# A gated cross-attention kernel on one Trainium2 core: the score operands' stacks filled inside SBUF instead of through DRAM, and the split of the negated maxima moved from VectorE to GpSimd

## The reference

```
x = x + tanh(g_xattn[0]) * xattn(layernorm(x), ctx, Wq, bq, Wk, bk, Wv, bv, Wo, bo)
x = x + tanh(g_ffn[0])   * ffn(layernorm(x), gate_up_packed, gate_up_scales, down_packed, down_scales)

# xattn: channels are split in 8 heads of 16, the 512 columns are the sequence
q, k, v = Wq x + bq, Wk c + bk, Wv c + bv        # per batch 128 x 512
q, k = rope(q, 8), rope(k, 8)                    # the first 8 channels of each head are rotated
p = softmax(q^T k / 4)                           # per head 512 x 512
out = Wo (p v) + bo
```

## Time and profile before

| | us |
|---|---|
| median of 3 runs | 924.72 (924.64 to 926.47) |
| the profiled execution: its time | 918.37 |
| its span | 916.6 |
| PE, DVE, ACT, POOL busy | 815.8, 522.1, 483.6, 178.5 |
| mean granted TensorE clock | 0.945 of full speed |

### The profile page before, as it was taken

One profiled execution on the slowest core, in us unless ns is written; L12 is line 12 of the kernel. 1 busy time (PEld: TensorE's weight loads), 2 busy tenths in 40 slices (PEclk: granted clock), 3 DMA queues, 4 the chain that ended last, 5 costly groups with the idle time before them and its releaser, 6 DMA issues. The chain is left out here.

```text
span 916.6 us, 13653 instructions
## 1 busy us (share of the span) xinstructions
PE 815.8 (89%) x5110; PEld 421.6 (46%) x5142; DVE 522.1 (57%) x760; ACT 483.6 (53%) x895; POOL 178.5 (19%) x174
## 2 busy tenths in 40 slices
PE   3378999999998988999993599999999999999997
PEld 1123333333333333334332376666666666666664
DVE  4398977888987867888871961314131423141113
ACT  2227776887787766778792552325231623252223
POOL 1232333333333423331112820000000000000000
PEclk8559999999999988999996889999999999999999
DMA  5678555666665666465212010002000110000001
GB/s 167 171 198 218 155 142 153 189 200 194 170 165 152 175 175 189 119 167 153 69 33 79 8 46 1 1 1 67 25 1 1 47 45 0 0 27 21 0 1 46
DMA packets 55176, 86.44 MB, mean 94 GB/s; under 512 B 19274, under 2 KB 20938, under 8 KB 55114
## 3 DMA queue, kind: packets, MB, share of 16 engines
q1 hardware_dynamic: 55114, 85.62, 33.0%
HBM read 44.70 MB, written 34.34 MB: 86 GB/s over the span
## 5 line engine op out<-in xcount | busy, mean ns | idle before, releaser
L670 DVE TENSOR_REDUCE neg_max<-s_ps 128x2 f32<-128x1024 f32 x256 | 310.0, 1219 | 61.8 <-PE s_ps L420 60.8
L536 ACT ACTIVATE probs<-st_ps 128x512 f32<-128x512 f32 x512 | 277.9, 597 | 105.5 <-PE st_ps L432 101.2
L448 PE MATMUL pv_ps<-probs,v_ones 128*32 128x256 f32 x2048 | 166.1, 397 | 12.6 <-ACT pv_sb L542 12.6
L1098 PE MATMUL gu_ps<-x_head,gu_head 128*128 128x512 f32 x352 | 155.9, 443 | 0.0
L965 DVE TENSOR_TENSOR hidden<-gu_ps,silu 128x512 f32<-128x512 f32 x44 | 30.4, 691 | 202.6 <-ACT silu L1040 202.6
L420 PE MATMUL s_ps<-k_stack,q_stack 48*128 48x512 f32 x512 | 135.4, 526 | 10.5 <-DVE neg_max L670 8.4
L1099 PE MATMUL gu_ps<-x_rest,gu_head 128*128 128x512 f32 x352 | 139.0, 395 | 0.0
L1040 ACT ACTIVATE silu<-gu_ps 128x512 f32<-128x512 f32 x44 | 26.3, 597 | 204.8 <-PE gu_ps L1101 204.8
L432 PE MATMUL st_ps<-q_stack,k_stack 50*128 50x512 f32 x512 | 110.6, 421 | 12.9 <-DMA q_stack<-max_scratch 12.7
L420 PEld LDWEIGHTS s_ps<-k_stack,q_stack 48*128 48x128 f32 x512 | 50.4, 193 | 121.1 <-issue 81.1
L1115 PE MATMUL y_ps<-dn_head,h_head 128*128 128x512 f32 x176 | 101.5, 577 | 1.1 <-DVE h_rest L967 1.0
(11 more groups left out here) (114 smaller groups left out, 807.1 us busy)
## 6 DMA issues: line engine op xcount, KB each, us to landing
q_stack<-image SPq DMA_DIRECT2D x64, 192.0 KB, 3.9
k_stack<-image SPq DMA_DIRECT2D x64, 192.0 KB, 4.5
image<-split_head SPq DMA_DIRECT2D x32, 256.0 KB
image<-split_head SPq DMA_DIRECT2D x64, 128.0 KB
image<-split_rest SPq DMA_DIRECT2D x32, 256.0 KB
ct<-ctx_dram SPq DMA_DIRECT2D x16, 256.0 KB, 5.5
swap<-proj SPq DMA_DIRECT2D x64, 64.0 KB, 2.0
scale_of<-inverse_scratch SPq DMA_DIRECT2D x16, 256.0 KB
```

The costliest lines, as they stand in the source:

```text
L448: last = nc.tensor.matmul(pv_ps[2 * KC * j:2 * KC * (j + 1), cols], v_ones[b % 2][:, kt, j, quad, :], probs[at % PROBS][:, j, cols], start ...
L536: nc.scalar.activation(probs[at % PROBS][:, tile % 4, :], st_ps[item % ST_BANKS][:], ACT.Exp).then_inc(st_read, 1)
L670: nc.vector.tensor_reduce(neg_max[j // 2][:, :, j % 2, qt], s_ps[item % S_BANKS][:], AXIS_X, ALU.max, negate=True).then_inc(s_read, 1)
L1098: nc.tensor.matmul(gu_ps[t % 2][:, half], head, x_head[:, k], start=(k == 0), stop=False)
```

## The change

`image` goes. `swap` and `turned` become 128 x 2 x 512 and cover q and k as whole tiles: the tables of cosine and sine have ones and zeros for channels that are not rotated, and `by_cosine`, `by_sine` and `split_rests` on GpSimd work on 1024 elements a partition. `split_heads` is one cast of 1024 elements on DVE at slot 4. The stacks (now three of them, q and k in one tile) are filled by `build_stacks`: six DMAs from `split`, each from 64 partitions to 16. The projections are q and k with all 128 columns, after slots 9 and 12; v's is at slot 5. The maxima's head and rest are made by `split_max` on GpSimd, and the transposes stand after slot 11 (`h = 0`, before: 7) and slot 1 (`h = 1`, before: 0). `merge_quads` is one DMA (before: four), `store_inverse` one (two), `load_inverse` two (one).

```diff
-X_TILES, C_TILES, PROBS = 8, 4, 3
-MIX_AT, ROT_AT, PASS_AT, V_AT = 1, 2, 5, 8
+X_TILES, C_TILES, PROBS, STACKS = 8, 4, 3, 3
+MIX_AT, HEADS_AT, V_AT, Q_AT, K_AT = 1, 4, 5, 9, 12
+Q_REST, Q_HEAD, K_HEAD, K_REST = range(4)
+BLOCKS = ((Q_HEAD, K_HEAD), (Q_HEAD, K_REST), (Q_REST, K_HEAD))
...
+            def fill_stacks(sp, n, blocks):
+                stack = stacks[n % STACKS]
+                for at in blocks:
+                    q, k = BLOCKS[at]
                     for odd in two:
+                        rows = stack[STACK * odd + KC * at:STACK * odd + KC * (at + 1)].bitcast(F32)
+                        pair = split[STACK * odd:STACK * (odd + 1), q:k + 1:k - q, :].bitcast(F32)
+                        sp.dma_start(rows.rearrange("c j w t -> c (j w t)"), pair).then_inc(stack_in[n % STACKS], 16)
+
+            def build_stacks(sp, n):
+                if n >= STACKS:
+                    sp.wait_ge(st_full, last_weight(n - STACKS, 1))
+                sp.wait_ge(heads, n + 1)
+                fill_stacks(sp, n, (0,))
+                sp.wait_ge(rests, n + 1)
+                fill_stacks(sp, n, (1, 2))
...
             def sync_step(sp, b):
-                nxt, proj_n = b + 1 < B, b + AHEAD_PROJ
-                if nxt:
-                    load_half(sp, b + 1, 1)
+                nxt = b + 1 < B
                 store_max(sp, b, 1)
-                if proj_n < B:
-                    swap_partners(sp, proj_n)
                 if b:
                     gather_sums(sp, b - 1, 1)
+                load_max(sp, b, 1)
+                if b:
                     merge_quads(sp, b - 1)
-                load_max(sp, b, 1)
-                if b >= 2:
-                    store_x(sp, b - 2)
-                if b:
                     store_inverse(sp, b - 1)
-                if proj_n < B:
-                    store_head(sp, proj_n, 1)
                 if b + 2 < B:
-                    load_half(sp, b + 2, 0)
+                    build_stacks(sp, b + 2)
                 if nxt:
                     store_max(sp, b + 1, 0)
                 if b:
                     load_inverse(sp, b - 1)
-                if proj_n < B:
-                    store_rest(sp, proj_n, 1)
-                if b + 5 < B:
-                    load_inputs(sp, b + 5)
+                if b + 4 < B:
+                    load_inputs(sp, b + 4)
                 if nxt:
                     load_max(sp, b + 1, 0)
+                if b >= 2:
+                    store_x(sp, b - 2)
                 gather_sums(sp, b, 0)
-                if proj_n < B:
-                    store_head(sp, proj_n, 0)
-                    store_rest(sp, proj_n, 0)
+                if b + AHEAD_PROJ < B:
+                    swap_partners(sp, b + AHEAD_PROJ)
...
+            def split_max(pool, n, h):
+                pool.wait_ge(s_read, S_NO["score", n, (h + 1) * SLOTS // QUADS - 1] + 1)
+                if n:
+                    pool.wait_ge(max_line[h], n)
+                maximum = neg_max[h][:].rearrange("p o j k -> p (o j k)")
+                nc.gpsimd.tensor_copy(max_rows[h][:, 0], maximum).then_inc(max_head[h], 1)
+                pool.wait_ge(max_head[h], n + 1)
+                nc.gpsimd.tensor_tensor(max_rows[h][:, 1], maximum, max_rows[h][:, 0].bitcast(F32), ALU.subtract).then_inc(max_rest[h], 1)
...
             def pool_step(pool, b):
+                split_max(pool, b, 1)
+                if b + 2 < B:
+                    by_sine(pool, nc.gpsimd, b + 2)
+                if b + AHEAD_PROJ < B:
+                    normalise(pool, nc.gpsimd, b + AHEAD_PROJ)
+                if b + 2 < B:
+                    split_rests(pool, nc.gpsimd, b + 2)
+                if b + 1 < B:
+                    split_max(pool, b + 1, 0)
                 if b >= 2:
                     residual(pool, nc.gpsimd, b - 2)
-                if proj_n < B:
-                    rotate(pool, nc.gpsimd, proj_n)
-                    rest_pass(pool, nc.gpsimd, proj_n)
-                if b + 4 < B:
-                    normalise(pool, nc.gpsimd, b + 4)
-                if proj_n < B:
-                    rest_rot(pool, nc.gpsimd, proj_n)
                 if b:
                     scale_heads(pool, nc.gpsimd, b - 1)
+                if b + AHEAD_PROJ < B:
+                    by_cosine(pool, nc.gpsimd, b + AHEAD_PROJ)
```

More of the change, by code:

```diff
@@ L120, in attend @@
         proj = sb("proj", [P, 2, T], F32)
[L121 to L127, removed]
+        swap, turned = sb("swap", [P, 2, T], F32), sb("turned", [P, 2, T], F32)
+        split = sb("split", [P, 4, T], F32R)
+        stacks = [sb(f"stacks{n}", [P, PAIRS, 2, T], F32R) for n in range(STACKS)]
+        v_ones = [sb(f"v_ones{p}", [P, KT, QUAD, V_WIDTH], F32) for p in two]
         probs = [sb(f"probs{n}", [P, QUAD, T], F32) for n in range(PROBS)]
@@ L175, in attend @@
         rotated = sem("rotated")
[L176 to L181, removed]
+        heads = sem("heads1")
+        rests = sem("rests1")
+        stack_in = [sem(f"stack_in{n}") for n in range(STACKS)]
         max_head = [sem(f"max_head{h}") for h in two]
@@ L185, in attend @@
         max_out = [sem(f"max_out{h}") for h in two]
-        max_in = [[sem(f"max_in{p}{h}") for h in two] for p in two]
+        max_in = [[sem(f"max_in{n}{h}") for h in two] for n in range(STACKS)]
         pv_done = sem("pv_done")
@@ L216, in swap_partners @@
             def swap_partners(sp, n):
-                sp.wait_ge(st_read, ST_NO["rot", n] + 1)
+                sp.wait_ge(st_read, ST_NO["k", n] + 1)
                 if n:
[L219 to L243, removed]
-                    for odd in two:
-                        rows = stack[p][STACK * odd:STACK * odd + DATA_ROWS, columns(h), :].bitcast(F32)
-                        heads = slice(odd * PAIRS + 2 * h, odd * PAIRS + 2 * h + 2)
-                        sp.dma_start(rows, image[n, row0:row0 + DATA_ROWS, heads, :]).then_inc(half_in[p][h], 16)
+                    sp.wait_ge(rotated, n)
@@ L257, in load_max @@
                     row = STACK * odd + DATA_ROWS
-                    sp.dma_start(q_stack[n % 2][row:row + MAX_ROWS, columns(h), :].bitcast(F32).rearrange("r j t -> r (j t)"),
-                                 max_dram[n, h, :, odd].rearrange("r i e -> r (i e)")).then_inc(max_in[n % 2][h], 16)
+                    sp.dma_start(stacks[n % STACKS][row:row + MAX_ROWS, columns(h), 0, :].bitcast(F32),
+                                 max_dram[n, h, :, odd].rearrange("r (j i) e -> r j (i e)", j=2)).then_inc(max_in[n % STACKS][h], 16)
             def gather_sums(sp, b, h):
@@ L413, in score @@
                 j, qt = score_of(slot)
-                p = n % 2
-                if slot % (SLOTS // QUADS) == 0:
-                    pe.wait_ge(half_in[p][j // 2], HALF * turn(n))
+                p = n % STACKS
+                if slot == 0:
+                    pe.wait_ge(stack_in[p], STACK_LOADS * stack_turn(n))
                 out = s_bank(pe, ("score", n, slot))
@@ L419, in score @@
                     rows = slice(STACK * odd, STACK * odd + DATA_ROWS)
-                    last = nc.tensor.matmul(out[:, odd, :], q_stack[p][rows, j, qt * P:(qt + 1) * P], k_stack[p][rows, j, :],
+                    last = nc.tensor.matmul(out[:, odd, :], stacks[p][rows, j, 0, qt * P:(qt + 1) * P], stacks[p][rows, j, 1, :],
                                             start=True, stop=True)
@@ L431, in weigh @@
                     out = st_bank(pe, ("weight", b, 2 * slot + odd))
-                    nc.tensor.matmul(out[:], k_stack[p][rows, j, kt * P:(kt + 1) * P], q_stack[p][rows, j, :],
+                    nc.tensor.matmul(out[:], stacks[p][rows, j, 1, kt * P:(kt + 1) * P], stacks[p][rows, j, 0, :],
                                      start=True, stop=True).then_inc(st_full, 1)
@@ L485, in _ @@
                 for n in (1, 2):
[L486 to L487 removed]
+                    for which in "qk":
+                        project(pe, n, which)
                 pe.wait_ge(scales_f32, 2)
```

284 lines of the change are left out of this document (116 added, 168 removed).

## The result

The changed kernel takes 1049.6 us (median of 4 runs, 1046.8 to 1059.7) against 925.6 of before on the same chip: 1.1345 times as long, 95% interval 1.1257 to 1.1433. The forecast was 1012. The profiled execution took 1049.55 us, 131 more than that of before; its mean granted clock is 0.882 (before 0.945). Some executions of a kernel are more than 1.5% slower than its fastest, at a lower granted clock: a median here is over all runs, a ratio and its interval leave these out.

What follows compares the result with a forecast made beforehand. PE, 89% busy, was taken as the bound, losing time to maxima delayed in DMA queues. Profiled 918.4 + 83 (steps) + 5 (start) + 1 (last two) - 2 (end) = 1005.4, plus 6.35 to the median: 1012 us; range 920 to 1060.

Steps and rivals of the forecast that it cites:

- The baseline: Step before the change: 27.1 us on the mean, 25.7 where PE waited for no maxima; `weigh` waits 29.2 in all.
- The fill: DMA fill of a stack, 16 partitions a transfer: 13.4 us at 117 GB/s after 1.1 to data flow, ending at 29.5.
- The rival that partitions don't bind: Stack fill: 16 partitions are as good, fill 6.7 us, step 25.7, kernel faster at 897 us; chance 0.16.
- Store of the maxima behind the fill: SP's queue: the maxima's store lands 1.4 us after the fill, at 30.9 us from `weigh` of slot 0.
- The load: Load of the maxima behind 768 KB of `scale_of`, `xt` and `ct`: 2.6 us taken, making the step 33.5.
- My last sign: Step above 33 with a fill of 13: loads of reciprocals and inputs, or GpSimd's list, were priced too low.
- The clock: PE idles about 5 us a step, so its clock falls to 0.50; cold slots up to the reciprocal cost 2.8 us.
- Rival 2: The fill is slow but PE's clock stays up: 30.7 us a step, 975 us in all; chance 0.16.
- The count of steps: Main loop: 13 steps, each 33.5 us against 27.1, 6.4 more a step, +83 us.
- The last two steps: Final two steps, which issue no fills but begin with a cold clock: +1 us.
- The start: Kernel start: first score stays near 39.36 us, `weigh` begins at about 66 where before 60.66; +5 us.
- At no cost: DVE, PE projections and GpSimd's longer operations (12.8 us of a 27 us step) and maxima split: hidden, adding nothing.

Runs made afterwards that it cites:

- spread: Changed kernel with `scale_of` loaded by four transfers of 16 outermost source rows to 32 partitions each, in place of two with 4 to 64: 1013.3 us.
- stride3: Changed kernel with the fill's six transfers writing their 16 rows to every third partition instead of 16 neighbours, same bytes: 978.2 us.
- load_first: Changed kernel with the load of the `h = 0` maxima issued directly behind their store, ahead of the loads of reciprocals and inputs: 1061.0 us.
- before_first: Kernel before the change, with the load of the `h = 0` maxima issued directly behind their store: 950.0 us, ratio 1.0223 to before.
- before_quiet: Kernel before the change, with the maxima's load directly behind their store and the loads of half a stack behind both: 952.3 us, ratio 1.0303.
- combo_first: Changed kernel with fill to every third partition, four `scale_of` transfers, fill ahead of reciprocals' store, and maxima's load directly behind their store: 939.9 us, ratio 1.0162.

## Why the prediction was right, and where it was off

The sign, the mechanism and its place were as forecast; the size was short by 38 us. In profiled executions: 131.2 us more, where the sum had 87. By its steps:

- **The baseline: read wrongly, with no effect on the sum.** The step of 25.7 us isn't "the one" without a wait for the maxima: the earlier trace rows counts 9 such waits of PE in 13 steps, so four had none (26.2, 25.7, 25.3 and 23.6 us, by the transposes). And its 29.2 us add PE's 12.7 to the 16.5 of the weight load, which runs beside it. The sum uses only the mean of 27.1.
- **The fill: its rate right, its end 1.3 us late.** 13.4 us at 117 GB/s were forecast; it ran at 118. From its issue to the landed stack were 16.1 us (292.40 to 308.53) for 14.5, so the stack was in 30.8 us after `weigh` (277.69 to 308.53) for 29.5. The rival that partitions don't bind falls, by this rate and by the 171 to 188 GB/s that other partitions gave.
- **The way to the fill: right.** Reciprocal 13.9 us after `weigh` (14.1), store 0.34 (0.6).
- **Store of the maxima behind the fill: its place right.** Its load is issued at 30.65 us (30.9). That these agree is in part luck: the store landed with the fill and not 1.4 us behind it, which makes good the 1.3 above.
- **The load: the term that was mis-sized.** "I take 2.6, as those 768 KB have had 1.4 us to drain": it took 5.4, 2.8 us more in each waiting step. I priced `scale_of` by its bytes, though the change had given it a new form, two transfers in place of one. That the form of this load is the cause is shown by `spread`, in which the same bytes hold the load up for 2.8 us, near the 2.6 that I took. My last sign had named it: a step above 33 with a fill of 13.
- **The clock: right.** PE stands 8.2 us (forecast 5), the clock falls to 0.50, and the slots up to the reciprocal take their cold time each step. Rival 2 falls. The idle time alone doesn't say when it falls: in `stride3`, at 276.71, PE had stood 3.58 us, went on with 0.51 us a pair, and the granted clock fell to 0.50 in the microsecond after.
- **The count of steps.** The first of the 13 steps had no wait: its stack isn't queued behind a reciprocal. Twelve cost 9.3 us more than the 27.1 and one 2.4 less, together +109 for +83.
- **The last two steps: wrong by 9.5.** I gave them +1, as they issue no fill. But the step that ends at 587.19 still waits for the last one and took 34.1 us, 10.5 more than its like before (23.6, from the transposes of that kernel at 427.71 and 451.28).
- **The start: right.** `weigh` begins at 66.56 (about 66). The rest of the start and the end, which the later slot of the transposes moves against each other, come to +5.6 for -2. I haven't taken these 7.6 apart.
- **The offset.** 6.35 us were added because before's profiled execution was under its median; this time the two agree within 0.1.

These are 26 + 9.5 + 1 + 7.6 = 44 us too little, and 6.35 too much: 38. The result lies 10 us inside the slow end of my range, but that end was set for a fill at 94 GB/s; that other terms, and not the fill, brought it there is luck. "At no cost" held: the split can be moved back to VectorE with no effect that can be told, and GpSimd's operations of 1024 elements took 2.36 us (2.56 taken). GpSimd's 237.6 us of waiting for `scale_of` held nobody up, until `load_first` made it later.

## What to carry to other kernels

Saving bytes and a trip through DRAM gained nothing here, since the path is set by time in the queues: cost a transfer by the partitions it writes and by its form (how many transfers, and with what outermost dimension), before its bytes, and recost those whose form changes by the way. A small transfer on the critical path pays for what is ahead of it, in another queue too, so look there first. Before an issue is moved ahead of others, ask who waits for these: four such moves (`load_first`, `before_first`, `before_quiet`, `combo_first`) lengthened the kernel that they started from, or at best left it the same.

## What was not expected of the hardware

A block of 16 rows written to every third of 46 partitions went at 171 to 188 GB/s, the same block to 16 neighbouring ones at 118. An 8 KB load took 5.4 us behind two broadcasts of 128 KB each and 2.8 behind the same bytes in four transfers. A store in a queue of its own took 13.5 us beside a fill and three kinds of loads that had been issued earlier in another one, and landed 5.8 us after the fill, as if it had been behind them all.
